# Gated attention with a routed two-expert network on one core: smaller groups for the prologue's powers, steps of the plan moved by fractions, and the gate of each tile on GpSimd

## The reference, cut to what matters

```
xn = layernorm(x)                                     # x: 8 batches, 512 tokens, 128 wide
# attention on xn: 8 heads of 16, q k v with biases
attn = softmax(q k^T / 4)
a    = attn v1 - lam * (attn v2)                      # v1, v2: lower and upper half of the heads of v
s    = (0.2 * layernorm(a) * ln_w + ln_b') Wo + bo
# routed network on xn: 8 experts, 128 -> 512 -> 128
h    = int(xn[:, 0] + xn[:, 1]) mod 8                 # truncated toward zero
y    = sum over e in {h, h+1 mod 8} of 0.5 * (relu(xn W1[e] + b1[e]) W2[e] + b2[e])
out  = x + s * silu(y)
```

## Time and profile before

| | |
|---|---|
| median of three executions | 422.58 us |
| profiled execution, whole | 423.16 us |
| its span (first to last instruction) | 421.3 us |
| TensorE busy | 389.6 us, 92% |
| VectorE busy | 300.1 us, 71% |
| ScalarE busy | 268.5 us, 64% |
| GpSimd busy | 153.2 us, 36% |

### The profile page before, as it was taken

One profiled execution on the slowest core, in us unless ns is written; L12 is line 12 of the kernel. 1 busy time (PEld: TensorE's weight loads), 2 busy tenths in 40 slices (PEclk: granted clock), 3 DMA queues, 4 the chain that ended last, 5 costly groups with the idle time before them and its releaser, 6 DMA issues.

```text
span 421.3 us, 8389 instructions
## 1 busy us (share of the span) xinstructions
PE 389.6 (92%) x2575; PEld 249.2 (59%) x2576; DVE 300.1 (71%) x793; ACT 268.5 (64%) x667; POOL 153.2 (36%) x188
## 2 busy tenths in 40 slices
PE   4986979999999999999999999999999999999984
PEld 1343868655676657666665668666666657663322
DVE  6797886667687766866676768766686767766884
ACT  3571556666667765577765767576665668575783
POOL 7753302172235442374335421642353232420100
PEclk9997799999999999999999999999999999999997
DMA  7974763244305640235504540344255141214840
GB/s 243 343 226 116 196 217 90 75 112 140 133 13 167 197 143 14 77 109 160 186 16 130 173 137 18 128 137 157 61 163 172 25 161 49 78 19 127 299 165 25
DMA packets 36946, 54.76 MB, mean 130 GB/s; under 512 B 6724, under 2 KB 25141, under 8 KB 36903
## 3 DMA queue, kind: packets, MB, share of 16 engines
q1 hardware_dynamic: 31456, 46.94, 33.5%
q0 software_dynamic: 3296, 6.76, 7.6%
q10 hardware_dynamic: 2151, 0.53, 0.6%
HBM read 15.59 MB, written 6.75 MB: 53 GB/s over the span
## 4 chain that ended last, share of the span: by engine, by line
PE 76%; DVE 11%; ACT 4%; issue 4%; DMA 2%; POOL 2%; DVEq 0%; ACTq 0%; POOLq 0%
PE ring L1383 14%; PE ring L1404 14%; PE pv_bank L1317 13%; PE score L1279 13%; PE exp L1304 11%; DVE neg_max L1034 4%; PE ring L1241 2%; PE ring L1343 2%; PE ring L1266 2%; PE ring L1325 1%; ACT hT L813 1%; ACT xin L775 1%; DMA qs<-max_rows 1%; DMA xs<-xn_rows,inverse 1%; PE ring L1365 1%
## 5 line engine op out<-in xcount | busy, mean ns | idle before, releaser
L1034 DVE TENSOR_REDUCE neg_max<-score 128x1 f32<-128x512 f32 x256 | 170.7, 685 | 70.2 <-PE score L1279 65.3
L1279 PE MATMUL score<-ks,qs 96*128 96x512 bf16 x256 | 98.4, 388 | 8.6 <-DVE neg_max L1034 7.4
L775 ACT ACTIVATE xin<-exp 128x512 f32<-128x512 f32 x120 | 70.1, 604 | 39.0 <-PE exp L1304 36.2
L1304 PE MATMUL exp<-qs,ks 99*128 99x512 bf16 x244 | 91.8, 380 | 3.2 <-ACT xin L775 1.5
L813 ACT ACTIVATE hT<-ring,pair 128x128 f32<-128x128 f32 x256 | 73.5, 375 | 28.1 <-PE ring L1383 25.4
L775 ACT ACTIVATE probs<-exp 128x512 f32<-128x512 f32 x124 | 72.8, 611 | 28.3 <-PE exp L1304 26.9
L679 POOL DMA_INDIRECT y_rows<-y_sb,inverse x32 | 32.0, 999 | 137.8 <-DVE y_sb L1166 136.6
L1404 PEld LDWEIGHTS ring<-w_sb,hT 128*128 128x128 f32 x568 | 74.2, 193 | 8.7 <-issue 2.1
L1404 PE MATMUL ring<-w_sb,hT 128*128 (+1 forms) x568 | 76.4, 278 | 0.8 <-ACT hT L813 0.8
L1383 PEld LDWEIGHTS ring<-xsT,pair 128*128 128x128 f32 x512 | 65.1, 191 | 13.8 <-issue 7.9
L1383 PE MATMUL ring<-xsT,pair 128*128 128x128 f32 x512 | 69.4, 278 | 0.5 <-issue 0.5
(11 more groups left out here) (195 smaller groups left out, 409.3 us busy)
## 6 DMA issues: line engine op xcount, KB each, us to landing
pair<-table SPq DMA_DIRECT2D x32, 580.0 KB
qs<-parts SPq DMA_DIRECT2D x42, 128.0 KB
ks<-parts SPq DMA_DIRECT2D x42, 128.0 KB
xin<-_attn_hidden_states_dram SPq DMA_DIRECT2D x8, 256.0 KB, 5.5
table<-in_L_ffn_W_dram SPq DMA_DIRECT2D x2, 1024.0 KB, 9.8
w_sb<-in_L_ffn_W_dram SPq DMA_DIRECT2D x8, 256.0 KB, 6.1
xn_rows<-xn SPq DMA_DIRECT2D x8, 256.0 KB, 3.1
table<-_attn_hidden_states_dram SPq DMA_DIRECT2D x8, 256.0 KB, 4.7
```

The costliest lines, as they stand in the source:

```text
L775: a.activation(prob(n), exp_banks[n][:, :], ACT.Exp, scale=SCALE).then_inc(exp_done, 1)
L1034: v.tensor_reduce(neg_max[:, b % 2, col:col + 1], score_bank[n % 2][:, :], AX.X, ALU.max, negate=True).then_inc(max_taken, 1)
L1279: t.matmul(score_bank[n % 2][:, :], qs[0:MAX_ROW, b % STK, hh, c * P:(c + 1) * P], ks[0:MAX_ROW, b % STK, hh, :], start=True, stop=True).t ...
L1304: t.matmul(exp_banks[n][:, :], ks[0:KROWS, b % STK, hh, kc * P:(kc + 1) * P], qs[0:KROWS, b % STK, hh, :], start=True, stop=True).then_inc ...
```

## The change

The groups of the power become (0,1), (1,2), (2,4), (4,6), (6,8), each with a time of its own. For all groups but the last the shift is made on GpSimd: minus the mean before the power, times rstd after it. VectorE only makes the shift of the last group, and ahead of it adds the first two columns of x for all tokens; the routing then multiplies that sum by rstd and adds twice the shift, two operations where there were three.

The gate of a tile leaves VectorE. GpSimd waits for tanh, adds 1 in place, waits for that, and multiplies with y.

Many times in the plan are moved: the extra tiles start earlier (8.4 to 7.6) and closer (2.6 to 2.3), the regular ones at 27.33 instead of 27.6, their gathers are issued 6.66 steps ahead instead of 6, their start rows 1.5 instead of 1, and the steps on either side of attention by up to 0.85.

```diff
-LN_GROUPS = ((0, 1), (1, 3), (3, 6), (6, 8))
+LN_GROUPS = ((0, 1), (1, 2), (2, 4), (4, 6), (6, 8))
-SHIFT_AT = (-58.5, -56.5, -51.5, -50)
+SHIFT_AT = (-58.5, -57.5, -55.5, -53.5, -50)
-EXTRAS_AT = 5.7
-GROUPS_AT = (9.05, 11.05, 13.05, 14.05)
+EXTRAS_AT = 5.2
+GROUPS_AT = (9.05, 10.72, 13.05, 14.05)
-FFN_FIRST = 8.4
-EXTRA_PACE = 2.6
-STATIC_FIRST = 27.6
+FFN_FIRST = 7.6
+EXTRA_PACE = 2.3
+STATIC_FIRST = 27.33
-INIT_AHEAD = 1
-H1, D0, D1 = 1.5, 3.3, 4.5
+INIT_AHEAD = 1.5
+H1, D0, D1 = 1.8, 3.3, 4.5
-SPLIT_MAX, TURN_MAX = 16.6, 19.3
-EXP_OFF, PV_OFF = 0.2, 3.5
-NORM_O, TURN_Z, PROJECT_O = 42.6, 41.5, 45.5
-LAMBDA_AT = 19
-FOLD_AT = 21
-TANH, GATE = 0.7, 1.7
+SPLIT_MAX, TURN_MAX = 16.8, 18.9
+EXP_OFF, PV_OFF = 0.05, 4
+NORM_O, TURN_Z, PROJECT_O = 41.76, 40.67, 45.16
+LAMBDA_AT = 18.67
+FOLD_AT = 20.5
+TANH, GATE = 0.7, 1.84
-LOAD_Y_AT = 249
+LOAD_Y_AT = 250.2
-                at(qkv + 5 + 4 * i, "split", b, i)
-        at(32 * b + LAG - 27.8 if b else FOLD_AT + 6.2, "values", b)
+                at(qkv + 5.4 + 4 * i, "split", b, i)
+        at(32 * b + LAG - 28.3 if b else FOLD_AT + 6.2, "values", b)
-            at(16 * grp + LAG + 20, "copy_o", grp)
-            at(16 * grp + LAG + 22.2, "turn_o", grp)
+            at(16 * grp + LAG + 19.17, "copy_o", grp)
+            at(16 * grp + LAG + 22.03, "turn_o", grp)
-        at(t - 6, "load_x", f)
+        at(t - 6.66, "load_x", f)
# GpSimd
                     pool.wait_ge(stats_ready, end)
+                    if end < B:
+                        g.tensor_scalar(shift[:, tok], mv[:, tok, 0], -1.0, None, ALU.mult)
                     link(g.tensor_scalar(var_eps[:, tok], mv[:, tok, 1], EPS, None, ALU.add))
                     g.tensor_tensor(rstd[:, tok], var_eps[:, tok], neg_half[:, 0:C * (end - first)],
                                     ALU.pow).then_inc(rstd_ready, 1)
+                    if end < B:
+                        pool.wait_ge(rstd_ready, s[1] + 1)
+                        g.tensor_tensor(shift[:, tok], shift[:, tok], rstd[:, tok], ALU.mult).then_inc(shift_ready, 1)
+                elif kind == "gate":
+                    tile = s[1] - NX
+                    pool.wait_ge(tanh_ready, tile + 1)
+                    link(g.tensor_scalar(tanh[:, :], tanh[:, :], 1.0, None, ALU.add))
+                    g.tensor_tensor(y_sb[:, tile % YB, :], tanh[:, :], y_sb[:, tile % YB, :],
+                                    ALU.mult).then_inc(gate_ready, 1)
# VectorE, routing
-                two = cmp[:, 0:2 * NT].rearrange("p (t k) -> p t k", k=2)
-                link(v.tensor_tensor(two, xin[:, :, 0:2], rstd[:, :].unsqueeze(2).to_broadcast([P, NT, 2]), ALU.mult))
-                link(v.tensor_tensor(two, two, shift[:, :].unsqueeze(2).to_broadcast([P, NT, 2]), ALU.add))
-                link(v.tensor_tensor(v01[:, :], two[:, :, 0], two[:, :, 1], ALU.add))
+                dve.wait_ge(pair_summed, 1)
+                link(v.tensor_tensor(v01[:, :], v01[:, :], rstd[:, :], ALU.mult))
+                dve.wait_ge(shift_ready, len(LN_GROUPS))
+                link(v.scalar_tensor_tensor(v01[:, :], shift[:, :], 2.0, v01[:, :], ALU.mult, ALU.add))
# VectorE, shift
+                    if end < B:
+                        continue
                     tok = slice(C * first, C * end)
+                    v.tensor_tensor(v01[:, :], xin[:, :, 0], xin[:, :, 1], ALU.add).then_inc(pair_summed, 1)
                     dve.wait_ge(rstd_ready, g + 1)
# VectorE, gate
-                elif kind == "gate":
-                    tile = s[1] - NX
-                    dve.wait_ge(tanh_ready, tile + 1)
-                    v.scalar_tensor_tensor(y_sb[:, tile % YB, :], tanh[:, :], 1.0, y_sb[:, tile % YB, :],
-                                           ALU.add, ALU.mult).then_inc(gate_ready, 1)
```

More of the change, by code:

```diff
@@ L381, in gated_attention_moe @@
         shift_ready = sem("shift_ready")
+        pair_summed = sem("pair_summed")
         b1_loaded = sem("b1_loaded")
```

## The result

The changed kernel took 411.62 us, the median of four executions (409.93 to 411.75); the kernel before took 422.50 beside it. The ratio is 0.973 [0.9708, 0.9753]: 2.7% faster, 10.9 us, where 4.0 us were forecast and at most 7.4 lay in the range. The direction was right and the size was not. The profiled execution has a span of 409.6 us, 11.7 less than that of the kernel before (421.3).

The account below looks back on a forecast made before the run. TensorE, busy 92%, was taken to bound the middle, so only its gaps or the two ends could give time. Gains 1.6 + 0.5 + 1.2 + 0.3 + 0.4 = 4.0 us gave 419.2 us (median 418.6), range 415.2 to 422.6.

Parts of the forecast that it names:

- Part 3: Middle: the new order has five instead of seven gaps of scores waiting for maxima behind "down"; 1.2 us gain, at most 2.5.
- Part 1: Head: shifts on GpSimd and a shorter routing bring routing, inverse table and first gather 1.6 us sooner, bounds 0.8 and 1.9.
- Part 2: Seven extra tiles, started earlier and closer, recover some TensorE idle time from 46.8 to 61.8 us: 0.5 us, at most 2.7.
- Rival 2: TensorE's low-clock stretch around the first tiles: half as long again, 420.8 us, chance 0.08; without it, 414.2 us, chance 0.05.
- Part 5: Tail: x reload and y's loads come 1 to 3 us sooner, ending the wait for last maxima; 0.4 us, at most 0.65.
- Part 4: Middle: the gate moves from VectorE to GpSimd, takes 1.0 us there and gains 0.3 us, at most 1.
- The slack of 0.8: Middle: a gather is used 5.5 us after issue against a slowest seen of 4.78, covering a gate up to 0.7 us later.
- the first rival: GpSimd's queue in the middle: late gathers hold TensorE at 12 splits, 8.4 us lost, giving 427.0 us; chance 0.10.
- Rival 3: Head gain held to 0.8 and the new order has as many gaps: 421.8 us, no measurable change; chance 0.13.
- three signs of being wrong: TensorE waiting for gathers behind 100 us, a low clock beyond 11 us, or the first gather not a microsecond earlier.
- The five bounds of gain: Largest gains of the five parts, head to tail: 1.9, 2.7, 2.5, 1.0 and 0.65 us, giving 413.8 us.
- the small head gain: Lower bound of the head's gain, 0.8 us, with half lost to GpSimd's extra operations; with the losses it gave 424.0 us.

Follow-up runs that it names:

- the extras group alone: Kernel before with only the head of the plan moved (extra tiles from 7.6 at pace 2.3, extras, groups 1, lambda, fold): 420.40 us, ratio 0.9972.
- the first four experiments: Gate alone 422.40 us, all moved times alone 411.60, new prologue alone 418.69 (each against the kernel before); changed kernel with gate back on VectorE 410.38.
- last series: On one chip beside the kernel before: changed kernel 412.03 us, ratio 0.9756; the same with the gate back on VectorE 412.42 us, ratio 0.9773.
- the exps and pv alone: Kernel before with one line changed, EXP_OFF 0.2 to 0.05 and PV_OFF 3.5 to 4: 419.37 us, ratio 0.9953.
- the attention group alone: Kernel before with only the steps beside attention moved (maxima, output's turn, norm, projection, values, splits, load of y): 419.33 us, ratio 0.9937.
- the tiles with it: Kernel before with both the regular tiles' places and the steps beside attention moved: 415.94 us, ratio 0.9852.
- The plan without its attention group: Kernel before with all moved times except those of the steps beside attention, old prologue, gate on VectorE: ratio 0.9970.
- the plan without the maxima's moves: Kernel before with all moved times, old prologue, gate on VectorE, but split and turn of the maxima back at 16.6 and 19.3: ratio 0.9869.
- the tiles group alone: Kernel before with only the regular tiles' places moved (start 27.33, second hidden 1.8, start rows 1.5, gathers 6.66, gate 1.84): 421.47 us, ratio 1.000.

## Why the prediction was wrong in size

**What bounds the kernel** held: TensorE's order. But the step after it, that only what takes away one of those gaps or shortens the two ends can shorten the run, did not hold. The step took 7.6 us of visible idle time as all that the middle could give. In the stretch between two "project" matmuls 3.05 us went, 0.73 of it visible. I compared start distances of neighbouring matmuls afterwards: taking for each pair of kinds the distance that four in five reach or exceed, and leaving rare pairs out, the lateness in this stretch was 10.1 us before and 7.0 after, where the idle time shows 4.7 and 3.9. It is an estimate, and another choice of pairs gives 10.7 and 7.8 or 11.4 and 8.4; but the difference, some 3 us each time, is the gain. That is the measure which should have bounded Part 3.

**Part 1, the powers**, was right in mechanism. The power starts 1.27 us sooner (forecast 1.25), the absolute value is 1.72 sooner, the inverse table starts 1.34 sooner (30.97), the first turn 1.23 (36.39 against 37.62). Forecast was 1.6, alone it measured 2.4 (1.2 to 3.6), and 2.0 between executions of like mean clock.

**Part 2, the extra tiles**, was taken at 0.5. The idle time behind the clock's stretch fell by 1.7, and the extras group alone measured 1.2 us (0.1 to 2.3), inside the plan 2.1, give or take 2.9. The value of 0.5 looks too low, but lies in both; the bound of 2.7 held.

**The clock.** Rival 2 had the stretch at the lower level longer or gone. It was shorter, and that needs nothing of the change: with the gate alone, which touches nothing ahead of tile 7's gate, the first stretch of the earlier trace rows looks like this, and tile 7 comes at 71.88 instead of 73.69:

```profile
37.60:46.80 9.20, 8.06 (x47) 6.25 (x48) 7.21 (x14) 3.91 (x15) 3.01 (x3) 0.80 0.80 199
```

Priced as in the forecast, by half of TensorE's busy time in it, the stretch took 4.4 us before (8.7 busy) and 2.2 after (4.4 busy). So of the 11.7 us between the two spans about 2.2 are this, and 0.5 more are the clock in the tail (Part 5).

In the medians it is less. In the series of the first four experiments the executions of the kernel before with a mean clock of 0.99 or more have a median of 420.3 us (five), the others 421.6 (thirteen). The changed kernel with the gate on VectorE has 410.2 and 411.2 (two each): about 10.2 us less at like clocks. Whether the change also makes the long stretch rarer is open. In the last series all ten executions of the changed kernel and its variant have mean clocks of 0.989 to 0.992, and eight of the kernel before 0.984 to 0.989.

**Part 3, the order in the middle**, is the step that failed: 1.2 us forecast, at most 2.5. The exps and pv alone gave 2.0 us, the attention group alone 2.7 (with the tail), and the tiles with it another 3.6. I looked at one pattern only, a score behind a "down". The count was fair as far as it went: seven such places in the order before and five after, and waits for maxima fell by 2.5 us. It left out the exps' waits for ScalarE (2.4 us before, none after; the 1.5 for `xin` are gone with the exps and pv alone), and what the order costs by itself. And it missed the second queue in the same order, the three banks: the order before had its own near miss at tile 31, and which groups may be moved together is decided there. The plan without its attention group has the same five places, and gains only 0.3% where the plan gains 2.2. So the step's method, a count of one kind of gap, could not tell the two apart.

**Part 4, the gate.** Its cost on GpSimd was right: 1.0 us was forecast and 1.3 to the store, measured are 1.07 and 1.35. The slack of 0.8 was wrong: it came from one gather of 4.78 us, but a chain of the changed kernel shows another of 5.69, and with the gate alone one issued 5.22 us ahead was 1.58 too late. So the first rival's mechanism is real, at 2 tiles, and cost 1.2 to 1.5 us with the old times. In the changed kernel the sign is as forecast (0.4 us, forecast 0.3), within the noise. TensorE's one wait for a gather in its middle is 0.6 us, at 129 us (tile 14):

```profile
PE ring L1375 <- DMA xs<-xn_rows,inverse: 0.6, 1, 0.6
```

As for the rules of the Trainium skill that stood beside this part: GPSIMD Engine Reference, Engine selection, has GpSimd about two times slower with two inputs and near line rate with one. The rows have 0.46 and 0.54 for the halves against 0.281 for the whole on VectorE, so the half with one input is the slower one here; the measurement decides. Of the lock between the two engines' SBUF operations that the Trainium skill states (SBUF — State Buffer, "SBUF: two separate sides") the gate's 32 adds show little, 0.532 to 0.580 us.

That the earlier gathers (6.66 ahead instead of 6) pay for the later gate fits this, but no run with just these two was made.

**Part 5, the tail.** The wait of 0.65 us for the last maxima is gone, as forecast, and it is back (1.0 us) in the plan without the maxima's moves, so the mechanism held. Behind tile 38 the tail is 1.3 us shorter instead of 0.4. The last exp starts 0.75 us sooner relative to tile 38 (410.13 before, 398.99 after), and from there to the end it takes 10.63 us instead of 11.13. This 0.5 is not the change: with the gate alone, whose last steps are the old ones, it takes 10.63 too. The last eight matmuls, in the kernel before at a granted clock of 0.50 and with the gate alone at 1.00:

```profile
415.41 2.07 PE L1343 MATMUL ring<-wo_eff,zT 128*128 128x128 f32 x8 [0.26 <-ACT zT L800]
```

```profile
414.44 1.16 PE L1344 MATMUL ring<-wo_eff,zT 128*128 128x128 f32 x8 [0.26 <-ACT zT L806]
```

**Rival 3** (all absorbed) fell. What the forecast said would show it right did show: no waits between statistics, under ten waits for maxima and under 5 us, last maxima on time. All of it was true of a gain more than twice as large, so it tested parts of the mechanism and not the size. Of the three signs of being wrong one showed as well: TensorE waited for a gather behind 100 us, once, 0.6 us, without the loss that it stood for.

**The range.** The five bounds of gain added gave 413.8 us, and 411.6 was measured: the bound of Part 3 is the one that was too low. The losses were also added wrongly: with the small head gain they give 426.0 and not 424.0, which made no difference here.

## What to carry to other kernels

When a change reorders steps around a bound engine, list every resource that is handed round in that order (here the score's two banks, the ring's three, the gathers' queue) and count the near misses of each in the old and the new order, before giving a size. Bound the gain by how late matmuls start against their own quickest spacing, not by visible idle time, and compare what the two orders cost at that spacing. Before two single profiles are compared, look at the clock in both. Small moves of neighbouring groups should be tried together: alone, a good move can measure as nothing, because it swaps a "down" with the projection and puts a held bank in the next tile's way.

## What the runs showed of the hardware

- A matmul of 512 columns is shown 0.38 us long while the next can start 0.22 later; TensorE's busy time for the same 2576 matmuls fell by 8.1 us, some 3 of them by the clock.
- A pv's first matmul starts 0.31 us behind an exp's and 0.17 behind a turn of the maxima.
- GpSimd's in-place add on a 128x128 tile of 32 bits takes 0.536 us, its product of two such tiles 0.457, and a transfer that waits for the product starts 0.28 us later.
- Gathers of 128 rows took 4.8 (before) and 4.9 us (after) from issue for the first, and 5.7 for one in the middle (after).
- The stretch at the lower clock around the first gather's landing was 10.2 or 6.8 us in executions whose work there was the same (the kernel before, the gate alone), and 3.4 in one of the kernel with the tiles group alone.
